# Transposed scores four slots behind the scores instead of five, in a two-layer transformer kernel on one core

## The reference

```
# layer 0 (condition -> shift, scale, gate through silu(cond) @ Wada + bada)
xm = layernorm(x, g1, be1) * (1 + sc_a) + sh_a
q, k, v = split(xm @ Wqkv)
x = x + gt_a * (softmax(causal(q k^T / 4)) v @ Wproj + bproj)
xm = layernorm(x, g2, be2) * (1 + sc_m) + sh_m
x = x + gt_m * (gelu(xm @ W1 + b1) @ W2 + b2)
# layer 1: the same without gates; all keys but the padded ones instead of the causal mask
```

## Time and profile before

| | us |
|---|---|
| median of 3 runs (lowest to highest) | 1189.88 (1187.13 to 1192.58) |
| the profiled execution | 1188.98 |
| its span, first to last instruction | 1186.9 |
| PE busy in the span | 1094.0 |
| PE weight loads busy | 959.8 |
| DVE busy | 747.9 |
| ACT busy | 624.0 |
| POOL busy | 253.1 |

### The profile page before, as it was taken

One profiled execution on the slowest core, in us unless ns is written; L12 is line 12 of the kernel. 1 busy time (PEld: TensorE's weight loads), 2 busy tenths in 40 slices (PEclk: granted clock), 3 DMA queues, 4 the chain that ended last, 5 costly groups with the idle time before them and its releaser, 6 DMA issues.

```text
span 1186.9 us, 24117 instructions
## 1 busy us (share of the span) xinstructions
PE 1094.0 (92%) x9228; PEld 959.8 (81%) x9228; DVE 747.9 (63%) x1627; ACT 624.0 (53%) x1255; POOL 253.1 (21%) x252
## 2 busy tenths in 40 slices
PE   3889999999999789999975899999999987999998
PEld 3778899998987578899874788888888765998997
DVE  5456666666665466655635777878777747556653
ACT  1146666666665633433422677767777676334431
POOL 5101221211211343223321121121211113111111
PEclk9789999999999998999987999999999999999999
DMA  7647767567661110000057554736547300001001
GB/s 214 113 67 113 131 107 119 102 106 117 145 97 30 19 41 9 10 9 14 15 88 151 85 80 69 95 60 88 77 75 92 57 2 1 19 20 35 19 19 36
DMA packets 50826, 81.49 MB, mean 69 GB/s; under 512 B 8916, under 2 KB 23476, under 8 KB 49620
## 3 DMA queue, kind: packets, MB, share of 16 engines
q1 hardware_dynamic: 49752, 78.37, 37.9%
q10 hardware_dynamic: 960, 1.57, 1.2%
HBM read 22.64 MB, written 8.44 MB: 26 GB/s over the span
## 4 chain that ended last, share of the span: by engine, by line
PE 72%; SPq 9%; DMA 9%; DVE 4%; issue 3%; ACT 2%; POOL 2%; ACTq 1%; POOLq 0%; DVEq 0%
PE st_bank L541 13%; PE g_bank L541 11%; SPq L406 8%; PE o_bank L541 8%; PE s_bank L541 7%; PE o_bank L629 7%; DMA k_stack<-qk_split 5%; PE s_bank L590 3%; PE s_bank L596 3%; PE st_bank L615 3%; DMA k_stack<-mask_dram 3%; PE st_bank L611 2%; PE st_bank L609 2%; PE s_bank L592 2%; PE g_bank L687 2%
## 5 line engine op out<-in xcount | busy, mean ns | idle before, releaser
L807 ACT ACTIVATE probs<-st_bank 128x384 f32<-128x384 f32 (+1 forms) x512 | 276.6, 547 | 152.6 <-PE st_bank L611 83.2
L541 PE MATMUL st_bank<-qk_split,q_stack 128*128 128x512 f32 x768 | 190.1, 406 | 14.4 <-ACT probs L910 9.8
L910 ACT ACTIVATE probs<-st_bank,cols 128x512 f32<-128x512 f32 x128 | 88.0, 689 | 219.4 <-PE st_bank L541 193.8
L1099 DVE TENSOR_REDUCE maxima<-s_bank 128x2 f32<-128x512 f32 x256 | 168.8, 684 | 51.0 <-PE s_bank L596 50.8
L541 PEld LDWEIGHTS st_bank<-qk_split,q_stack 128*128 128x128 f32 x768 | 146.9, 194 | 52.7 <-ACT probs L910 13.1
L1095 DVE TENSOR_REDUCE maxima<-s_bank 128x3 f32<-128x384 f32 x256 | 136.8, 552 | 65.6 <-PE s_bank L592 62.1
L596 PE MATMUL s_bank<-k_stack,q_stack 97*128 97x256 f32 x512 | 117.1, 311 | 26.7 <-DMA k_stack<-mask_dram 14.5
L541 PE MATMUL g_bank<-xmT,wa 128*128 128x256 f32 x768 | 123.1, 300 | 4.8 <-POOL xmT L1271 4.8
L629 PE MATMUL o_bank<-probs,v_sb 128*32 128x256 f32 (+1 forms) x2048 | 123.4, 358 | 1.6 <-ACT probs L807 1.6
L596 PEld LDWEIGHTS s_bank<-k_stack,q_stack 97*128 97x128 f32 x512 | 78.8, 192 | 55.6 <-issue 41.5
L1271 POOL TENSOR_TENSOR xmT<-xm_full,xmT 128x512 fp32r<-128x512 f32 x32 | 42.2, 1320 | 332.2 <-ACT xmT L873 332.2
(11 more groups left out here) (114 smaller groups left out, 2129.5 us busy)
## 6 DMA issues: line engine op xcount, KB each, us to landing
q_stack<-qk_split SPq DMA_DIRECT2D x192, 128.0 KB, 4.4
k_stack<-qk_split SPq DMA_DIRECT2D x180, 128.0 KB, 6.2
gate_rows<-gate_dram SPq DMA_DIRECT2D x32, 128.0 KB, 3.0
w_dram<-w_in SPq DMA_DIRECT2D x8, 512.0 KB, 7.6
wm_f32r<-w_dram SPq DMA_DIRECT2D x4, 1024.0 KB, 8.4
out<-x_sb SPq DMA_DIRECT2D x8, 512.0 KB, 2.9
x_sb<-x_in SPq DMA_DIRECT2D x4, 512.0 KB, 7.9
k_stack<-qk_split ACTq DMA_DIRECT2D x12, 128.0 KB, 8.4
```

The source lines that it names most:

```text
L541: last = mm(dst, weights[i], rows[j], start=(f == 0 and n == 0), stop=(f == tiles - 1 and n == len(TERMS) - 1))
L807: activation(probs[:, h % 8, 0:n], st_bank[h % 2][:, 0:n], ACT.Exp, scale=SCALE)\
L910: activation(h_full[:, m % 2], st_bank[m % 2][:, :], ACT.Gelu, bias=cols[:, cb + m:cb + m + 1])\
L1099: v.reduce_max(maxima[:, gb.mod(2), 0:2, slot], bank[:].rearrange("p (i n) -> p i n", n=T), AX.X).then_inc(max_done, 1)
```

## The change

One constant:

```diff
-LAG = 5
+LAG = 4
```

## The result

| | before | after |
|---|---|---|
| median (lowest to highest) of 5 runs, us | 1189.88 (1187.13 to 1194.59) | 1178.39 (1174.40 to 1179.48) |
| ratio, 95% interval | | 0.9891 (0.9868 to 0.9915) |
| the profiled execution; its span, us | 1188.98; 1186.9 | 1178.39; 1176.2 |
| TensorE busy, us | 1094.0 | 1091.0 |
| TensorE at half clock (1.2 GHz) within the span, us | 61.7 | 69.0 |

The kernel is 1.1% faster, 11.5 us, where 5.9 were forecast. Two more chips gave 0.9895 (0.9878 to 0.9912) and 0.9868 (0.9845 to 0.9891). One run of the kernel before, among 29 on the chip of the first four kernels tried, took 3588.83 us and is left out of every ratio as a slow one.

The account below looks back on a forecast made before the run. TensorE was taken to set the pace nearly everywhere (72% of the chain), transfers in places. Terms: -9.0 + 0.5 + 0.3 + 1.6 + 0.55 + 0.1 = -5.95, from 1189.88 to 1184.0 us; range 1180.5 to 1190.

Parts of the forecast that it names:

- 5.2 forecast: Sign in layer 1: q's restack issued 5.2 us after a step's first scores instead of 6.4.
- waits of L596 for k and mask: Scores waiting for restacked k rows or mask row: none left from the fourth step of layer 1 on.
- the rule of the Trainium skill that was weighed against the change: All DMAs share 16 engines and interleave, so the restack could reach into the maxima's transfer time; nothing added for it.
- the third rival: First transposed product of a batch: maxima land late because the restack is in flight; slower, 1199 or 1214 us; chance 0.08.
- the step from 732.29: Layer-1 step of 20.40 us taken to have no pause, and as the pattern for all steps.
- Layer 1's margin: First transposed product against the maxima's landing: margin 0.50 us, afterwards 0.02; 0.04 in twelve steps, 0.5 us cost.
- Layer 0's late landing: Maxima landing after 2.6 us instead of 2.15 would make the first transposed product wait 0.2; two such steps, 0.3 us.
- The exposed waits: Last step with scores of each layer: first transposed product already waits for the maxima; 0.61 us more in layer 0, 0.48 in layer 1.
- The drain: Step where scores have ended: one more transposed product ahead of the previous batch's transposes and projection; 0.31 and 0.24, 0.55 us.
- Moving the groups: Group products and ACT copies one slot earlier: costed at nothing; without ACT's cover, 28 steps pay up to 0.4 us each.
- the 7.3 counted: Nine layer-1 waits of scores for k rows or mask row, 3.9 + 3.4 us, all taken as gained.
- the late landing: One layer-1 maxima landing of 3.4 us, where TensorE already waited, was to wait 0.48 us longer.

Follow-up runs that it names:

- the restack held: Changed kernel, but SyncE waits for one transposed product more, so q's restack starts where it did before: 1.0023 (1.0001 to 1.0044) of the kernel before.
- experiment 4: Changed kernel with ACT issuing the maxima's second transfer (0.9887 of before), lag five for the last two batches (0.9871, 0.9868), both (0.9891), or lag five in layer 0 (0.9902).
- groups alone: Kernel before with lag still five, only the four group products and their ACT copies moved to slots 9, 13, 1 and 5: 1.0027, again 1.0014.
- the lag of three: Changed kernel with the lag cut from four to three, group products in slots 8, 12, 0 and 4: 1281.76 us, 1.0744 (1.0705 to 1.0783) of the kernel before.

## Why the prediction was right and wrong

**Right: the mechanism.** q's restack starts 5.10 us after the head of a step (5.2 forecast). All waits of L596 for k and mask are gone from the fourth step of layer 1 on; with the restack held they are back. The maxima did not land later for the restack in flight: 2.1 in the median in both layers. So the rule of the Trainium skill that was weighed against the change (DMA: Bandwidth & Descriptors, Issuing engines are not separate DMA queues), and the third rival with it, do not show in these small transfers with 0.47 us of restack behind them; of two small transfers issued at once one did land later (experiment 4).

**Wrong: the floor of a layer-1 step.** The step that failed is the reading that "the step from 732.29 ran 20.40 us with no pause at all", and "That step is the pattern for all." It had a pause, nearly all of it covered by the busy time (the earlier trace rows has 20.37 us busy of 20.40). TensorE at the head of that step of the kernel before, and at the head of a step of the changed kernel:

```profile
731.40 0.88 PE L541 MATMUL g_bank<-wa,attnT 128*128 128x256 f32 x6
732.32 0.48 PE L596 MATMUL s_bank<-k_stack,q_stack 97*128 97x256 f32 x2
732.63 0.40 PE L615 MATMUL st_bank<-q_stack,k_stack 99*128 99x256 f32 x2
```
```profile
787.63 0.88 PE L541 MATMUL g_bank<-wa,attnT 128*128 128x256 f32 x6
788.35 0.41 PE L596 MATMUL s_bank<-k_stack,q_stack 97*128 97x256 f32 x2
788.60 0.40 PE L615 MATMUL st_bank<-q_stack,k_stack 99*128 99x256 f32 x2
```

From the projection's start to the first scores it is 0.92 us before and 0.72 after, from there to the transposed scores 0.31 and 0.25: 0.26 us in one step. The six projection matmuls show as 0.88 long in both, though the next instruction can start after 0.72; a wait of 0.16 us lies under their end, and the 0.04 beyond it is too short for a line of the waits. The records say what was waited for: the last k transfer landed 0.09 us ahead of that head, as it did at five more of the thirteen heads from the fourth step on, one with a wait of 1.1 us among them; in the changed kernel it landed 0.23 to 1.50 us ahead. The kernel before shows it by itself, too. In its second profile the last k transfer landed 0.40 us ahead of one head, and the intervals there are 0.72 and 0.24:

```profile
880.52 0.88 PE L541 MATMUL g_bank<-wa,attnT 128*128 128x256 f32 x6
881.24 0.40 PE L596 MATMUL s_bank<-k_stack,q_stack 97*128 97x256 f32 x2
```

Step by step the busy time fell by 0.2 to 0.3 us in nine of the twelve, by 0.5 in two and by 0.1 in one: together the 3.5 us. The floor of a layer-1 step is 20.15 us, not 20.40. The Trainium skill (Perfetto Trace Analysis, Tensor Engine Instruction) says that the profiler works out a matmul's end from its size and does not observe it; these rows agree, and show what follows for a floor read off busy time.

**Wrong in size, the small terms.** Layer 1's margin cost nothing (+0.5 forecast), although the landing now sets the start of the weight load in every step: that wait is too short to move the matmul behind it. Layer 0's late landing cost 0.6 once (+0.3 forecast). The exposed waits went from 1.15 to 1.70 us in layer 1 and from 0.78 to 1.53 in layer 0, so they grew about as forecast (0.55 and 0.75 for 0.48 and 0.61). The drain did not: without any half clock the end of attention 1 took 46.3 us in the changed kernel on the second chip, against 46.6 and 47.0 before, where 0.7 more was forecast for it (0.48 and 0.24).

**Not in the sum at all: group products and clock.** Moving the groups was costed at nothing, with up to 0.4 us a step if ACT's cover were gone. It took 0.06 us off each layer-0 step instead (0.7 us in twelve). And no term was for TensorE's clock: its stretches at half cost 1.7 and 3.4 us in the two ends of attention in the profile of the changed kernel, and 3.6 us net over the span (69.0 against 61.7 at half). It hid a part of the gain, so the forecast missed the gain in the steps by more than the total shows. By how much is loose: a second profile of the kernel before has 69.4 us at half clock, and two more of the changed kernel have 79.1 and 79.3.

**The account of the 5.6 us** (1184.0 forecast, 1178.39 measured): in the twelve layer-1 steps hidden waits 3.5, the margin 0.5, 0.7 of idle time beyond the 7.3 counted (8.0 are gone) and 0.5 for the late landing, which was to wait longer and did not recur; in the layer-0 steps 0.4 (1.8 measured against 1.4). That is 5.6. Against it, the ends of attention, the MLPs and the starts came to +5.0 - 2.4 = +2.6 in the profiles, where +1.6 and +0.1 were forecast. That leaves 4.7; the other 0.9 is between the two profiled executions (10.6 us apart) and the medians (11.5).

**Open.** Why a lag of four with a pair of groups unmoved is 0.4 to 0.9% slower than the changed kernel. In the profiles most of it is clock (6.1 of 7.8 us), two thirds of that in the end of attention 1, which ran at half for 7 to 17 us in all four such profiles and for 0 to 7 in those of the changed kernel, after the same exposed wait (1.4 to 2.3 us against 1.5 to 1.9). What in the work of that stage tips it was not found; nor is the loss of groups alone beyond doubt (0.27%, then 0.14% with an interval that includes none).

## What to carry to other kernels

A step in which an engine is "busy all the time" is no floor until the thing it might have waited for is seen to have landed well ahead: compare the intervals between starts with those of a place that can't wait. A transfer's issue hung on the last reader of a buffer is worth moving up even if the visible waits are small. And when a lag is cut, cut it until the other chain just sets the start of its reader without lengthening the step, and not a slot further. Count for each slot what changes sides with it: one slot more moved 1.0 us of group product ahead of the transposition with which that chain starts, and the wait was 2.1 us where 1.2 was expected.

## What the runs showed of the hardware

- Repeated waits cost twice. With one wait of 2.1 to 3.4 us in each of twelve layer-1 steps of 22.5 to 25.9 us, TensorE was granted half its clock for 41.0 us of them (20.5 us lost, beside 28.1 of waits); the changed kernel had none there. Over the span it was 163.7 us instead of 69.0.
- Transfers of the same 16 KB that land 2.15 us after their issue in nearly every batch take 2.4 to 3.5 us in the same few places of most kernels in which SyncE issues both: in the fourth of the twelve layer-0 steps (all but the lag of three), and in the last layer-1 step with scores (all but groups only, the held restack and the lag of three). What they meet there was not found.
- Two such transfers issued at once by two engines land 2.1 and 2.7 us after their issue; issued 0.6 us apart by SyncE they take 2.1 each.
- In each of the waits of over 0.3 us of a batch's first transposed product, 125 over all profiles, the weight load started 0.04 us after the last landing of the maxima. So a start that close behind a landing is to be read as a wait, even where the idle time shows none.
